# Two graph layers in one kernel: stores left running across stages, degrees and stores moved in the norm stage, a one-pass last stage

## What is computed

```python
src_h = h[src] @ W_msg.T + b_msg                 # layer 1
msg = src_h + edge_embed[clip(edge_type, 0, 8)]
messages = segment_sum(msg, dst)
x = layernorm(x + gru_cell(messages, x, W_ih, W_hh, b_ih, b_hh))

proj = x @ fc_weight.T                           # layer 2
el, er = proj[src], proj[dst]
e = sum(leaky_relu(el + er, 0.2) * attn, -1)
gate = sigmoid(sum(el * er, -1))
w = sigmoid(e * gate)
neigh = segment_sum(x[src] * w[:, None], dst) / maximum(deg, 1.0)[:, None]
x = layernorm(x + (1.0 + eps) * x + neigh)       # deg: edges into each node
```

## Time and profile before

| | us |
|---|---|
| median of 3 runs (lowest, highest) | 3278.78 (3277.06, 3279.28) |
| the profiled execution, own time | 3269.84 |
| its span, first to last instruction | 3268.0 |
| TensorE busy / VectorE / ScalarE / GpSimd | 2154.1 / 2508.1 / 1592.7 / 2135.2 |
| mean granted TensorE clock | 0.772 |

### The profile page before, as it was taken

The page is one execution under the profiler, slowest core; times in us unless marked ns, Lnnn a source line. Parts: engine busy times, 40 slices in busy tenths (PEclk is TensorE's granted clock), DMA queues, the critical chain, the costliest instruction groups (busy, mean ns, idle before and its releaser), DMA issues. The chain is left out here.

```text
span 3268.0 us, 64802 instructions
## 1 busy us (share of the span) xinstructions
PE 2154.1 (66%) x13842; PEld 1733.9 (53%) x13842; DVE 2508.1 (77%) x12778; ACT 1592.7 (49%) x3458; POOL 2135.2 (65%) x2191
## 2 busy tenths in 40 slices
PE   1399999999989745555555555555655555555653
PEld 1277777777754445454444454454555545545552
DVE  6577777777735678888888888888888888888877
ACT  2265555555543345445445454445454544544541
POOL 2456766667720067777777777777777777777772
PEclk9999999999999766667667667767566666676665
DMA  7222222222220465655555565665565565566562
GB/s 142 79 57 65 73 65 70 71 67 70 68 71 1 146 182 158 168 163 158 168 163 158 165 166 158 162 166 161 159 170 161 158 167 164 157 169 164 155 169 65
DMA packets 357854, 424.88 MB, mean 130 GB/s; under 512 B 174156, under 2 KB 242134, under 8 KB 357733
## 3 DMA queue, kind: packets, MB, share of 16 engines
q0 software_dynamic: 103728, 266.13, 29.7%
q1 hardware_dynamic: 251793, 156.64, 18.3%
q10 hardware_dynamic: 2212, 0.60, 0.1%
HBM read 399.44 MB, written 23.70 MB: 129 GB/s over the span
## 5 line engine op out<-in xcount | busy, mean ns | idle before, releaser
L1407 POOL DMA_INDIRECT got<-rows,idx x1624 | 1546.5, 952 | 538.7 <-issue 509.8
L1573 PE MATMUL sum_ps<-whot,got 128*128 128x128 f32 x3264 | 690.1, 381 | 642.3 <-DVE whot L1419 573.2
L1573 PEld LDWEIGHTS sum_ps<-whot,got 128*128 128x128 f32 x3264 | 594.0, 273 | 730.5 <-DVE whot L1419 641.0
L735 POOL DMA_INDIRECT got<-x_rows,idx x532 | 540.5, 1016 | 255.9 <-issue 161.2
L1566 PE MATMUL er_ps<-win,hot_t 128*128 128x128 bf16 x4932 | 528.6, 285 | 260.7 <-ACT hot_t L1517 238.4
L886 ACT CAST work<-c_ps 128x318 bf16<-128x318 f32 x1092 | 454.9, 431 | 398.7 <-PE c_ps L962 391.1
L1475 DVE CUSTOM_DVE_ANT_0 pr_s<-got,er_ps 128x128 f32<-128x128 f32 x1624 | 370.0, 283 | 363.8 <-DMA got<-rows,idx 357.9
L1566 PEld LDWEIGHTS er_ps<-win,hot_t 128*128 128x128 bf16 x4932 | 468.9, 133 | 303.6 <-ACT hot_t L1517 268.2
L913 PE MATMUL span_ps<-x_parts,work 128*126 128x393 bf16 x2756 | 611.4, 332 | 0.0
L1419 DVE TENSOR_SCALAR whot<-iota_f,dl,w_s 128x128 f32<-128x128 f32 x1632 | 459.0, 358 | 0.3 <-ACT w_s L1522 0.3
L1547 ACT ACTIVATE r_s<-er_ps 128x512 f32<-128x512 f32 x406 | 242.3, 597 | 373.2 <-DVE er_ps L1487 371.2
(11 more groups left out here) (239 smaller groups left out, 1879.3 us busy)
## 6 DMA issues: line engine op xcount, KB each, us to landing
work<-dst_row SPq DMA_DIRECT2D x413, 256.0 KB, 4.0
got<-rows,idx POOLq DMA_INDIRECT x1624
win<-parts SPq DMA_DIRECT2D x118, 96.0 KB
got<-x_rows,idx POOLq DMA_INDIRECT x532
idx<-src_rows SPq DMA_DIRECT2D x413, 2.0 KB, 4.0
parts<-split SPq DMA_DIRECT2D x13, 384.0 KB, 2.9
x_rows<-x_parts SPq DMA_DIRECT2D x1, 4641.0 KB
rows<-nodes SPq DMA_DIRECT2D x13, 256.0 KB, 3.1
```

The lines of the kernel that those rows point to most:

```text
L735: pool.indirect_dma_start(got[:, c, i, 0:3 * D], None, x_rows, bass.IndirectOffsetOnAxis(ap=idx[:, c, i:i + 1], axis=0)).then_inc(gathered ...
L1407: pool.indirect_dma_start(got[:, c, i, :], None, rows, bass.IndirectOffsetOnAxis(ap=idx1[:, c, i:i + 1], axis=0)).then_inc(gathered[c], 16)
L1573: mm = pe.matmul(sum_ps[:, 0:P], got[:, c, i, D:2 * D], whot[:, c, i, :], start=(c == 0 and i == 0), stop=(c == NS - 1 and i == STEP - 1))
```

## The change

- The waits of SP for the landing of its preparation stores move from the end of the preparation to SP's head of the counting block; GpSimd waits for those of them whose source lies in `sums` or `nodes` before it clears `sums`, which it now does after `counts`. To that end some preparation buffers move into `nodes` and `sums`, and the tables into buffers that outlive the block. The large `x_rows` store is cut in two, each half after its half of L552.
- `LEAD = 2`: two pairs without bodies run ahead of the rounds, none behind them. VectorE and TensorE wait for the memsets one pair later.
- The degree products and the degree division move from the gated update to the norm stage, seven tiles in each of the sets 5 to 12.
- `split` gets a buffer for every tile and lives on into layer 2. SP stores normed and projected rows of all sets first, then the parts of all sets, and waits for the parts only in layer 2, before the first window load.
- Scratch of layer 2 lies in `small_rows`. ScalarE multiplies `nodes` by `c_x` ahead of its loop there.
- The last stage makes one pass: per tile one operation mixes sum, degree and node; root, reciprocal and offset are made per set; ScalarE normalises sets 0 to 11, VectorE the last. The transposes have four buffers instead of two.

```diff
-                    sp.wait_ge(lo_cut, 2)
-                    sp.dma_start(x_rows[0:xf * LO, :].rearrange("(b p) f -> p b f", p=LO),
-                                 x_parts[0:LO, 0:xf, 0:3 * D]).then_inc(x_out, 16)
+                    for i, (b0, b1) in enumerate(half_b):
+                        bm = min(b1, xf)
+                        sp.wait_ge(lo_cut, i + 1)
+                        sp.dma_start(x_rows[b0 * LO:bm * LO, :].rearrange("(b p) f -> p b f", p=LO),
+                                     x_parts[0:LO, b0:bm, 0:3 * D]).then_inc(x_out, 16)
...
-                    sp.wait_ge(left_out, 16 * (2 + (br > 0)))
-                    sp.wait_ge(dst_out, 48)
-                    sp.wait_ge(tables_out, 48)
...
+                    sp.wait_ge(left_out, 16 * (2 + (CT % ROWS > 0)))
+                    sp.wait_ge(dst_out, 48)
+                    sp.wait_ge(tables_out, 48)
...
                     pool.memset(nodes[:, ft:NTL, :], 0.0).then_inc(nodes_set, 1)
+                    pool.memset(counts[:, 0:NPAD], 0.0).then_inc(zeroed0, 1)
+                    pool.wait_ge(left_out, 16 * (2 + (CT % ROWS > 0)))
+                    pool.wait_ge(dst_out, 48)
                     pool.memset(sums[:, 0:NPAD], 0.0).then_inc(zeroed0, 1)
-                    pool.memset(counts[:, 0:NPAD], 0.0).then_inc(zeroed0, 1)
-                    pool.wait_ge(x_out, 16 * (1 + (xr > 0)))
+                    pool.wait_ge(x_out, 16 * (2 + (xr > 0)))
...
+                            if g_first_added(k, h):
+                                dve.wait_ge(zeroed0, 3)
...
-                    dve.wait_ge(zeroed0, 3)
+                    for k in range(1, LEAD):
+                        make_pair(k, False)
                     with dve.Fori(0, ROUNDS) as r:
                         for p in range(ROUND):
-                            make_pair(ROUND * r + p + 1, False, p, r)
-                    with dve.Fori(ROUNDS * ROUND + 1, PAIRS) as k:
-                        make_pair(k, False)
+                            make_pair(ROUND * r + p + LEAD, False, p, r)
                     add_group(CGN - 2, base_of(CGN - 2))
...
-                            pe.matmul(deg_ps[:, tile:tile + 1], counts[:, tile * NODES:(tile + 1) * NODES],
-                                      ones[0:NT, :], start=True, stop=True)
...
-                    dve.tensor_scalar(rdeg[:], deg_ps[:, 0:NTL], 1.0, None, ALU.max).then_inc(stats_done, 1)
-                    dve.wait_ge(stats_done, NTL + 1)
-                    dve.reciprocal(rdeg[:], rdeg[:])
...
+        split = sb("split", [NODES, NTL, 3, D], BF16)
+        parts_out = sem("parts_out")
...
+            DEG = min(5, NQ - 1)
+            PER_DEG = -(-NTL // (NQ - DEG))
...
+                    dve.wait_ge(deg_done, NQ - DEG)
+                    dve.tensor_scalar(rdeg[:], deg_ps, 1.0, None, ALU.max).then_inc(deg_read, 1)
+                    dve.wait_ge(deg_read, 1)
+                    dve.reciprocal(rdeg[:], rdeg[:])
...
+                        if q >= DEG:
+                            if q == DEG:
+                                pe.wait_ge(d_copied, 1 + (last_m > 0))
+                            for tile in range((q - DEG) * PER_DEG, min((q - DEG + 1) * PER_DEG, NTL)):
+                                mm = pe.matmul(deg_ps[:, tile:tile + 1], counts[:, tile * NODES:(tile + 1) * NODES],
+                                               ones[0:NT, :], start=True, stop=True)
+                            mm.then_inc(deg_done, 1)
...
-                        act.wait_ge(parts_out[b], 16 * h + 16)
-                        act.copy(split[:, b, :, 0, :], p_ps[:, b, :, :]).then_inc(p_copied, 1)
+                        act.copy(split[:, bass.ds(q * QUAD, QUAD), 0, :], p_ps[:, b, :, :]).then_inc(p_copied, 1)
...
+                    def store_parts(h, b):
+                        q = h * 2 + b
+                        t = bass.ds(q * QUAD, QUAD)
                         sp.wait_ge(cut, 3 * q + 3)
-                        sp.dma_start(parts_q[:, t, :, :], split[:, b, :, :, :]).then_inc(parts_out[b], 16)
+                        sp.dma_start(parts_q[:, t, :, :], split[:, t, :, :]).then_inc(parts_out, 16)
 
                     each_quad(sp, store_quad)
...
+                    sp.wait_ge(parts_out, 16 * NQ)
...
+                    for q in range(NQ):
+                        t = slice(q * QUAD, (q + 1) * QUAD)
+                        act.activation(nodes[:, t, :], nodes[:, t, :], ACT.Copy, scale=c_x[:]).then_inc(scaled, 1)
...
+                    def root(q):
+                        act.wait_ge(agreed, QUAD * (q + 1))
+                        act.activation(rstd[:, q * QUAD:(q + 1) * QUAD], moments[:, q * QUAD:(q + 1) * QUAD, 1],
+                                       ACT.Sqrt, bias=low_bound[:]).then_inc(rooted, 1)
+                    def normalise(q):
+                        act.wait_ge(shifted, q + 1)
+                        for t in range(q * QUAD, (q + 1) * QUAD):
+                            act.activation(nodes[:, t, :], nodes[:, t, :], ACT.Identity, scale=rstd[:, t:t + 1],
+                                           bias=offset_s[:, t:t + 1]).then_inc(finished_act, 1)
+                    act.wait_ge(bound_set, 1)
+                    for q in range(NQ):
+                        root(q)
+                        if q >= 2:
+                            normalise(q - 2)
+                    normalise(LAST - 1)
...
+                    def scale_of(q):
+                        t = slice(q * QUAD, (q + 1) * QUAD)
+                        dve.wait_ge(rooted, q + 1)
+                        dve.reciprocal(rstd[:, t], rstd[:, t]).then_inc(inverse, 1)
+                        dve.wait_ge(inverse, q + 1)
+                        dve.scalar_tensor_tensor(out=offset_s[:, t], in0=moments[:, t, 0], scalar=-1.0,
+                                                 in1=rstd[:, t], op0=ALU.mult, op1=ALU.mult).then_inc(shifted, 1)
+                    dve.memset(low_bound[:], LN_EPS).then_inc(bound_set, 1)
+                    dve.wait_ge(scaled, NQ)
                     for q in range(NQ):
-                        t = slice(q * QUAD, (q + 1) * QUAD)
                         dve.wait_ge(m_turned, q + 1)
-                        dve.wait_ge(steps, S * q + 1)
-                        dve.tensor_tensor(mean_s[:], m_ps[:, q % 2, :, :],
-                                          rdeg[:, t].unsqueeze(2).to_broadcast([NODES, QUAD, D]), ALU.mult
-                                          ).then_inc(steps, 1)
-                        dve.wait_ge(steps, S * q + 2)
-                        dve.scalar_tensor_tensor(out=nodes[:, t, :], in0=nodes[:, t, :], scalar=c_x[:],
-                                                 in1=mean_s[:], op0=ALU.mult, op1=ALU.add).then_inc(steps, 1)
-                        dve.wait_ge(steps, S * q + 3)
                         for i in range(QUAD):
-                            dve.bn_stats(stats[:, i, :], nodes[:, q * QUAD + i, :]).then_inc(steps, 1)
+                            t = q * QUAD + i
+                            dve.scalar_tensor_tensor(out=nodes[:, t, :], in0=m_ps[:, q % 4, i, :],
+                                                     scalar=rdeg[:, t:t + 1], in1=nodes[:, t, :],
+                                                     op0=ALU.mult, op1=ALU.add).then_inc(mixed, 1)
                         for i in range(QUAD):
-                            dve.wait_ge(steps, S * q + 4 + i)
-                            dve.bn_aggr(moments[:, q * QUAD + i, :], stats[:, i, :]).then_inc(steps, 1)
-                    dve.wait_ge(steps, S * NQ + 1)
-                    dve.tensor_scalar(rstd[:], moments[:, :, 1], LN_EPS, None, ALU.add).then_inc(spread, 1)
-                    dve.wait_ge(spread, 2)
-                    dve.reciprocal(rstd[:], rstd[:]).then_inc(spread, 1)
-                    dve.wait_ge(spread, 3)
-                    dve.sem_inc(spread, 1)
-                    normalise(dve, range(0, HERE), finished)
-                @block.gpsimd
-                def _(pool):
-                    pool.wait_ge(spread, 4)
-                    normalise(pool, range(HERE, NTL), finished_pool)
+                            dve.wait_ge(mixed, q * QUAD + i + 1)
+                            dve.bn_stats(stats[:, i, :], nodes[:, q * QUAD + i, :]).then_inc(stated, 1)
+                        if q >= 1:
+                            scale_of(q - 1)
+                        for i in range(QUAD):
+                            dve.wait_ge(stated, q * QUAD + i + 1)
+                            dve.bn_aggr(moments[:, q * QUAD + i, :], stats[:, i, :]).then_inc(agreed, 1)
+                    scale_of(LAST)
+                    dve.wait_ge(shifted, NQ)
+                    for t in range(LAST * QUAD, NTL):
+                        dve.tensor_scalar(nodes[:, t, :], nodes[:, t, :], rstd[:, t:t + 1], offset_s[:, t:t + 1],
+                                          ALU.mult, ALU.add).then_inc(finished, 1)
...
```

115 lines of the change are left out of this document (57 added, 58 removed).

## The result

| | median of the runs, us | lowest to highest | profiled execution | its span |
|---|---|---|---|---|
| before | 3277.92 | 3272.57 to 3279.28 (4) | 3269.84 | 3268.0 |
| changed | 3242.27 | 3231.14 to 3248.43 (4) | 3231.14 | 3229.2 |

The ratio is 0.9891, with a 95% interval of 0.9876 to 0.9905: 35.7 us less. The forecast was 3257 us, 21.6 less. The direction and the range held; the gain was under-sized by a good third.

What follows compares the result with a forecast made beforehand. TensorE bounds counting and gated update, GpSimd's gathers layer 2, a VectorE chain the last stage. -6.4 + 7.5 - 20.2 + 0 + 10 + 1 - 13.5 = -21.6 us: 3248.2 profiled, 3257 as median; range 3240 to 3278.

Steps and rivals of the forecast that it cites:

- Preparation: Preparation stage: SP's dropped waits on landings free 3.2 us, the split x_rows store's earlier start 3.2; -6.4 us.
- rival A: End of preparation: counting does begin early as SP runs ahead of two half stores; some 23 us more gain, 3234; 6%.
- Counting: End of counting: without the lone pair as cover, TensorE waits for the last body's gathers; +7.5 us, bounds 4 and 11.
- Degrees out of the update: Gated update: TensorE saves 1.63 us in each of 11 sets and 2.3 in the thirteenth; -20.2 us.
- Degrees into the norm stage: Norm stage's last eight sets: seven tiles of degree products each, set comes out even at 3.8 us; 0, from -2 to +4.
- parts behind all rows: End of norm stage: parts drain after the last projected rows, so layer 2's first gather starts later; +10 us, bounds +5 and +14.
- Rival B: Norm stage: TensorE's clock is low, a set with degrees takes 6.7 us; 21 us more, 3278, no change; 12%.
- Scaling: Start of layer 2: ScalarE's 13 scalings delay sums, 1 us of 7 reaches GpSimd; +1 us, bounds 0 and 4.
- Last stage: Last stage in one pass: sets of 2.8 us, then a short end, no table loads; -13.5 us, bounds 10 and 17.
- C: Layer 2: the gather period rises, 13 ns each eat the whole gain, 20 ns give 3289 us; 7%.
- D: Parts and waiting gathers cost little, each at its lower bound; 3248 us, within the range; 10%.

Runs made afterwards that it cites:

- one_store: The changed kernel with its x_rows store in one piece again, after both halves are cut; 3245.35 us, ratio 0.9935 to the kernel before.
- deg_in_update: The changed kernel with the degree products back in the gated update and none in the norm stage; 3261.68 us, ratio 0.9974 to the kernel before.
- parts_between: The changed kernel with each set's parts stored right behind that set's rows again; 3222.09 us, ratio 0.9852 to the kernel before.

## Why the prediction was right and where it was off

**Preparation** (-6.4; measured -12.5). Right: SP stays held behind x_rows, and the small stores with it, so rival A fell; the waits on landings were worth what I took for them, 3.3 us (one_store: from the first table's issue to GpSimd's first clearing 4.1 us instead of 7.4). Mis-sized: "I give the pair the old 39 us"; a pair of halves takes 34 to 36, and its first half starts 3.9 earlier, all of which counts. That they take less was no part of the reasoning, and its cause is open. Expected to see the hold "for most of 40 us": seen, in two parts.

**Counting** (+7.5; measured +10.8). The mechanism was right: the pair was the last body's cover. Mis-sized was what comes behind the wait. The last index load was issued 0.4 us before the last column was done (908.70 against 909.07) and not 0.9; its gathers ended 30.1 us later (938.8) and not 29.1; TensorE had the rows 2.1 us after that end (940.90) and not 1.5. These are 2.1 us. I gave the last quarter 1.6 us and the clock 0.5; the quarter took 2.48 and the post behind it, at the same low clock, 0.9 more than before: 1.3 us. Together 3.4 us, where the table shows that I missed 3.3.

**Degrees out of the update** (-20.2; measured -24.9, against deg_in_update -24.6). Right: TensorE is the bound and the saving is whole. Mis-sized: 1.63 us per set. It was 1.84: the transposes leave 0.44 us between products and not 0.55, and the product ahead of them hands over 0.09 us sooner to a transpose than to a degree. Not foreseen: the one to three sets at the lower clock, which went away with the degrees.

**Degrees into the norm stage and parts behind all rows** (0 and +10; measured together +6.0). Rival B fell: the clock is 1.00 where the degrees are taken. Misread was the old set. The 3.78 us that I called even with the new one were an average over one set of 5.34, five of 3.82 at half the clock and two of 2.91; TensorE waited for ScalarE not 1.15 to 1.31 us in each, but 3.75 once and then 0.9. The new set took 3.17 us and not 3.8: seven tiles of degrees hold TensorE 1.65 us (1105.87 to 1107.52) and not 2.17, so 0.24 each where I had 0.31, and the rest is overlap of its neighbours. So the sets of the stage got shorter by 5.2 us together (2.2 the longest, 0.65 each of five, one longer by 0.26), where I had 0, and this is the mis-sized term. With about 10 for the parts, and the longer spell at the low clock in one of the two profiles, that gives the 6. What I said against B, that the fall came after ScalarE's wait and the wait is removed, was enough: by deg_in_update the clock stays up without the degrees. The rule of the Trainium skill that I had weighed against the row at 0.52 (TensorE: Matmul & The Clock Gate, Part 1: throttled is the default, activity releases) agrees with the 1.00 in a stretch where TensorE is busy 11.00 of 11.00 us, but these runs don't show that the added products were needed for it. The parts' drain was right: 14.2 us held, about 10 us on the path by parts_between.

**Scaling** (+1; +1.0 in the two pairs, +4 over all profiles). Right mechanism: ScalarE is late, so the sums are, so a gather is held. Mis-sized was what is left of 7 us. At the eighth chunk (the 29th gather) the sum that it waits for ended 6.8 us later after the first gather than in the kernel before. My slack of 5.1 takes away all but 1.7 of that, and the gather starts 0.8 us behind the end of the sum: 2.5 us reach GpSimd in the two changed profiles, up to 3.6 in others, and I had 1. Most of it is already paid at the seventh chunk (the 25th gather), which I didn't look at: GpSimd asks for a count of sums there, too (L1427), and the count starts at 5 (L1604), so the second sum of the loop releases it. The 1.0 of the two pairs is lower than these 2.5 because the mean gather of the changed pair was 1 ns shorter, which differs as much between executions of one kernel.

**Last stage** (-13.5; measured -18.0). I had a set at 2.8 us and it takes 2.35. The four operations on nodes take 1.01 us up to the statistics, where the two old ones took 1.51 with their handovers: 0.5 less, not 0.3. The next set no longer waits 0.46 us from the start of the aggregation, but 0.29. And reciprocal and product add 0.27 and not 0.4. That is 0.45 x 13 = 5.8 us, of which the end of the stage, longer than I had it, took 1.3 back. That no table is loaded between root and cheap function was right: one load in the stage. The rule that I had cited for it (the Trainium skill, ScalarE: Activation LUTs, section on table sets) agrees with that one row.

**Rivals.** C fell: the gather is 952 ns as before. D, each of the waiting costs at its lower bound, fell with the +10.8. In the profiles my forecast missed 19 us, in the medians 14. Three savings were taken low, by 6.1, 4.7 and 4.5 us, and the norm stage high by 4; 3.1 are the difference between executions in the counting, and the 3.3 of its end go the other way. In each of the four I let the old cost of a neighbouring step stand (the store's 39 us, the gap between products, the handovers of a set, the sets at half the clock) although the edit changes that step as well. So the range held in part by luck: preparation, update, norm-stage sets and last stage all lie outside their own bounds, all to one side, and the median of 3242 lies 2 us below what the bounds of the steps gave (3244 to 3270), 2 above the lower end of the range (3240).

## What to carry to other kernels

Ask of each store which instruction stands behind it in its queue: the last one issued lets its stage end, though it holds the first load of the next stage, and the same bytes in another order were worth 18 us here. A store is best issued beside computing that leaves the DMA engines idle, and a deferred one is paid where nothing is left to compute: some 10 us for 14 of them here. Before a set's time is carried over, look at what clock it ran at. Before a step is moved to the front of a loop, look at what it covered at the end.

## What the runs showed of the hardware that was not expected

- One store of 4641 KB held the issue behind it 38.8 to 39.0 us. With two stores of half of it each, 34 to 36 us passed from the first issue until the small store behind them was through (six profiles).
- A clearing by GpSimd of 5.63 us holds VectorE's operations on 16-bit columns for its whole length, also where it clears 9 partitions only, while the small f32 one ahead (0.23 us) ran; two clearings held it 10.54 us, one 4.96.
- TensorE's granted clock dropped to 0.5 for one to three of the thirteen sets of the update (11.18 us instead of 9.53, or 9.03 instead of 7.33) in each of the three profiles in which four one-column products stood between the transposes of a set, and in none of the ten without.
- In the norm stage the granted clock was 0.5 for 20 us after TensorE had stood idle for 3.75 us, with TensorE busy 14 of 20 us (before), and 1.00 without that idle time, with TensorE busy 10.9 of 20 (deg_in_update).
- The mean of 1624 gathers differs between executions by up to 3 ns (952 to 955), which moves layer 2: 2058.1 us at 952 and 2065.2 at 955, the ends of the ten profiles with scalings.
